# Two semaphores in turn for the second layer's gathers, each gather begun after the last but one has landed

## The reference, cut to what matters

```python
h = silu(edge_scalars @ Wfc1);  w = h @ Wfc2            # 192 weights of every edge
f0 = x0 @ Wl1_0;  f1 = einsum('num,uv->nvm', x1, Wl1_1) # 160 features of every node
e0 = f0[edge_src];  e1 = f1[edge_src]                   # the gather: a row of f for each edge
mid0 = w0 * e0 * sh0;   mid1 = w3 * (e1 . sh1);  mid2, mid3 = ...   # products
n0, n1, n2, n3 = segment_mean(mid, edge_dst)            # sums over the edges of a node
...                                                     # small products by node, layer norm
```

## Time and profile before

| | us |
|---|---|
| median of 3 runs | 6791.19 |
| lowest and highest of them | 6786.99, 6808.58 |
| span of the profiled execution | 6574.9 |
| PE busy (matmuls) | 4404.1 |
| DVE busy | 4082.6 |
| POOL busy | 3046.1 |
| ACT busy | 1176.2 |

### The profile page before, as it was taken

How to read it: one execution, slowest core, us unless ns; L and a number is a source line. 1 busy time by engine, 2 the same in 40 slices (tenths; PEclk the granted TensorE clock), 3 DMA queues, 4 the chain that set the end, 5 groups by cost and what they waited for, 6 DMA issues and landing times. The chain is left out here.

```text
span 6574.9 us, 113593 instructions
## 1 busy us (share of the span) xinstructions
PE 4404.1 (67%) x32521; PEld 3293.8 (50%) x32521; DVE 4082.6 (62%) x7506; ACT 1176.2 (18%) x3413; POOL 3046.1 (46%) x3249
## 2 busy tenths in 40 slices
PE   3767777777776777799776655655655665565555
PEld 2545555555555555689564434444444444444444
DVE  7877778778787766577455445444544544544544
ACT  0322222222222222000120111111111111111111
POOL 0556666566665666100035444444444444444442
PEclk7877778888788777899886666676666667666666
DMA  3333333333333333688332222222222222222221
GB/s 133 94 94 100 94 101 97 98 95 99 94 101 93 101 94 103 216 271 274 119 97 54 48 49 49 48 49 49 49 50 49 48 47 51 48 49 48 50 47 32
DMA packets 602395, 572.30 MB, mean 87 GB/s; under 512 B 183060, under 2 KB 491412, under 8 KB 602308
## 3 DMA queue, kind: packets, MB, share of 16 engines
q0 software_dynamic: 150528, 258.71, 14.5%
q1 hardware_dynamic: 414772, 227.28, 13.7%
q10 hardware_dynamic: 37008, 85.28, 4.2%
HBM read 412.44 MB, written 158.52 MB: 87 GB/s over the span
## 5 line engine op out<-in xcount | busy, mean ns | idle before, releaser
L2299 POOL DMA_INDIRECT q_fg<-f,q_index x1568 | 1484.1, 946 | 1608.8 <-DVE q_prod L2353 1138.1
L1026 POOL DMA_INDIRECT messages<-stage,place x1568 | 1506.8, 961 | 993.3 <-ACT stage L1237 506.4
L2546 PE MATMUL q_ps_m<-q_prod,q_onehot_sh 128*32 128x160 f32 x12544 | 914.4, 426 | 1015.6 <-DVE q_sums L2367 850.2
L1328 PEld LDWEIGHTS ps_m<-by_attr,turned 128*128 128x128 f32 x6272 | 1096.5, 226 | 281.3 <-issue 246.8
L2367 DVE SCALAR_TENSOR_TENSOR q_sums<-q_ps_m,split_q,q_sums 128x161 f32 x784 | 301.2, 384 | 1485.4 <-remote 1294.9
L1328 PE MATMUL ps_m<-by_attr,turned 128*128 128x160 f32 x6272 | 1204.7, 353 | 17.6 <-issue 13.0
L2546 PEld LDWEIGHTS q_ps_m<-q_prod,q_onehot_sh 128*32 128x32 f32 x12544 | 541.7, 150 | 1330.3 <-DVE q_sums L2367 908.4
L1298 PE MATMUL ps_y<-w_xy,xt 32*128 32x256 f32 (+3 forms) x1176 | 476.9, 705 | 488.0 <-ACT xz L1209 250.8
L2533 PE MATMUL q_ps_w<-q_wfc,q_hidden 64*128 64x192 f32 x3136 | 514.6, 425 | 206.6 <-DVE q_prod L2353 145.3
L1237 ACT COPY stage<-ps_m 128x320 f32<-128x320 f32 x784 | 337.2, 435 | 1737.9 <-PE ps_m L1328 848.1
L1118 DVE STREAM_TRANSPOSE by_attr<-by_node 128x2048 f32<-128x2048 f32 (+1 forms) x294 | 548.0, 1915 | 2.7 <-ACT by_node L1212 2.7
(11 more groups left out here) (247 smaller groups left out, 4487.3 us busy)
## 6 DMA issues: line engine op xcount, KB each, us to landing
nat<-in_edge_attr SPq DMA_DIRECT2D x392, 256.0 KB
rows_in<-messages ACTq DMA_DIRECT2D x208, 324.0 KB, 3.4
rows_in<-messages SPq DMA_DIRECT2D x208, 324.0 KB, 3.4
messages<-stage,place POOLq DMA_INDIRECT x1568
q_fg<-f,q_index POOLq DMA_INDIRECT x1568
messages<-zeros ACTq DMA_DIRECT2D x49, 324.0 KB, 2.2
q_a<-in_edge_attr SPq DMA_DIRECT2D x196, 64.0 KB
xw<-in_x SPq DMA_DIRECT2D x98, 80.0 KB
```

Source lines behind the costliest of these rows:

```text
L1026: nc.gpsimd.indirect_dma_start(out=msgs, out_offset=bass.IndirectOffsetOnAxis(ap=place[:, r, k:k + 1], axis=0), in_=stage[:, r, k, :], in_ ...
L1328: last = nc.tensor.matmul(ps_m[g % BANKS][:, k % 2 * D0:k % 2 * D0 + D0], turned[:, r, half, k * P:(k + 1) * P], by_attr[:, r, k, :, half] ...
L2299: nc.gpsimd.indirect_dma_start(out=fg[:, i, place_of(v), :], out_offset=None, in_=f_tab, in_offset=bass.IndirectOffsetOnAxis(ap=index[:, i ...
L2546: nc.tensor.matmul(ps_m[strip, 0:D0], oh_sh[:, strip], prod[:, h % 2, g * QUAD + place_of(v), 1 if c < 3 else 0, :], start=(v == 0), stop= ...
```

## The change

Two semaphores in place of eight, used in turn by the DMAs of a quad; each DMA waits until the one two before it has landed; the marker increment stands before each DMA; DVE and ACT wait for both semaphores, with counts that run through.

```diff
-            s_fg = [sem(f"fg{i}") for i in range(RING)]
+            INFLIGHT = 2
+            s_fg = [sem(f"fg{i}") for i in range(INFLIGHT)]
+            LANDS = 16 * (QUAD // INFLIGHT)
...
-                        pool.sem_inc(s_begun, 1)
                         for v in range(QUAD):
+                            reached(pool, s_fg[v % INFLIGHT], n * LANDS + v // INFLIGHT * 16)
+                            pool.sem_inc(s_begun, 1)
                             nc.gpsimd.indirect_dma_start(out=fg[:, i, place_of(v), :], out_offset=None, in_=f_tab,
-                                                         in_offset=bass.IndirectOffsetOnAxis(ap=index[:, i // 2, i % 2 * QUAD + v:i % 2 * QUAD + v + 1], axis=0)).then_inc(s_fg[i], 16)
+                                                         in_offset=bass.IndirectOffsetOnAxis(ap=index[:, i // 2, i % 2 * QUAD + v:i % 2 * QUAD + v + 1], axis=0)).then_inc(s_fg[v % INFLIGHT], 16)
...
-                        dve.wait_ge(s_fg[i], (t + 1) * (16 * QUAD))
+                        for landed in s_fg:
+                            dve.wait_ge(landed, (k * 2 + g + 1) * LANDS)
...
-                        for i in (2 * h, 2 * h + 1):
-                            reached(act, s_fg[i], t * (16 * QUAD))
+                        for landed in s_fg:
+                            reached(act, landed, (k - AHEAD + 1) * (2 * LANDS))
```

## The result

The changed kernel takes 6211.9 us (median of 4 runs, 6200.9 to 6217.9), the kernel before in the same comparison 6789.1 (6786.4 to 6808.6). The ratio is 0.9148, with a 95% interval of 0.9126 to 0.917: 8.5% faster, where slower was forecast. The profiled execution went from a span of 6574.9 to 6211.1 us, 363.8 us less.

What follows compares the result with a forecast made beforehand. Bound: the second layer's gather burst plus the chain behind it, PE's results coming at the latest with the last landing. Mean growth 1.69 us times 196 batches, 331 us, added to the median 6791.2 gave 7120; range 6420 to 7370.

Steps and rivals of the forecast that it cites:

- (1): Eight semaphores become two, with two waits each on DVE and ACT; taken as 0, 118 us at the most.
- (2): Marker increment on POOL moves from each quad to each gather, 1176 more sequencer instructions; taken as 0.
- (3): POOL's gather waits for landing of the one two before: 2.6 + 0.87 us, a pair 3.47 instead of 2.50.
- the 0.89 of the row: POOL's wake-up from a standing wait, read from message L2353's end to the gather's start; 0.87 us was used.
- Rival 2: POOL's wake-up is hidden, a pair takes 2.64 us; slower by 82 us at most, 6873; chance 0.09.
- rival 3: No change: no more than two or three gathers are under way, so the limit hardly binds; 6790; chance 0.06.
- (4): Second layer: PE stays late until the longer burst's last landing, 1.69 us per batch, 331 us; 7120, chance 0.48.
- rival 1: Second layer: pauses of 2.22 us free PE, batch falls to POOL's floor 13.88, 357 us less, 6434; chance 0.37.
- long batches: Second-layer batches of 18.79 us, whose add came with the last landing; claimed to grow by 2.91 us.
- short ones: Second-layer batches of 13.41 us, whose add came in mid-burst; claimed to grow only to POOL's floor, 0.47 us.
- 6950: Low end of the likeliest case: wake-up half hidden, pair of 3.0 us, long batches +1.5, short +0, 147 us.

Runs made afterwards that it cites:

- Four under way: The changed kernel with INFLIGHT 4 instead of 2, so each gather waits for the one four before; 5071.7 us, ratio 1.0025 to the kernel before.
- the bookkeeping stretch: Kernel before, second-layer rounds 8 to 14 of one execution, with an already-met wait and an extra increment ahead of each gather; 16.2 us a batch.

## Why the prediction was wrong

What bounds the kernel: right for the record, and only for sessions of its kind. "While gathers stream, PE's results are seen late" is what the runs confirmed; where it is not so, the same program takes 5059 us and POOL's 10.0 us a batch is the bound. That the trace of one execution can't tell this from a property of the program was not in the prediction at all.

(1) and (2), semaphores and increments at 0: right within what the runs can tell. Four under way costs 0.25% (13 us) where POOL is the bound; where PE is late the bookkeeping stretch is no faster than streaming.

(3), the price of the wait: right in size. A landing and a wake-up take 3.41 us (3.47), a pair 3.45 on the mean with 3.39 at the median (3.47), POOL's floor in the changed kernel is 13.79 (13.88). The wake-up is visible where it was disputed: with 2.6 us to the landing, 3.41 leaves 0.8 us, near the 0.89 of the row. The 50 ns that the Trainium skill gives ("DMA: Bandwidth & Descriptors", section "Anatomy of one DMA — SWDGE (gpsimd) path") are those of the sequencer's dispatch alone. They were no price for the whole way from a landing to the next gather's start, which is what the prediction used them for. Rival 2 is out by the same number, rival 3 by the pairs in the timeline.

(4), "held until the last landing", is the step that failed, and with it the choice between it and rival 1. Its arithmetic for a held batch is sound (570 us, the upper end of the forecast, when DVE was held in every batch), its premise is not: with the pairs, PE's results were not held, and DVE's waits for "remote" fell from 1295 us to 2.8. The split into long batches (+2.91) and short ones (+0.47), from which the 331 us came, was not tested. I decided between the two by one pause of 2.17 us in which PE crept on, and one of 2.68 in which it moved, as if the length of a single gap mattered. The gaps of the changed kernel are 2.1 us, the very length that I took for too short. But those of the earlier trace rows are single gaps in a stream of 1.25 us, the others come in each pair. In one execution a gap of 2.03 after each fourth gather fails and after each second succeeds, and by the table the mean spacing sorts the batches; the pairs' mean of 1.72 us lies over the boundary. The clue was in the prediction, as the last sentence of rival 1 (one gather under way where there had been two nearly all the time), and I gave it less weight than the two pauses. Two small slips changed nothing: the add of 5045.00 came just behind the start of the seventh gather (5044.98), so only the last had still to start, and 6791 + 147 is 6938, not 6950.

The size of rival 1 was right where its premises held: on the profiled span -357 us was computed and -364 came, in part by luck: the second layer gave -373, and +40 and -31 us came elsewhere. The predicted 6434 missed the measured 6211.9 for another reason: I added the difference to the median of 6791, which is 216 us above the time of the profiled execution. The changed kernel's median is within 1 us of its profiled run (6212.7). So the 216 us are not a constant around the span. The sessions with PE late gave the kernel before 6564.5, 6567.1 and 6762.6: it has two levels some 200 us apart, its profiled execution was at the lower and the timed runs of the record at the upper, and of the changed kernel only one level where PE is late is seen (6200.9 to 6217.9). Beside a kernel before of 6567 the same 6212 would be 5.4% faster instead of 8.5%, an estimate from two sessions. What makes the upper level is open.

The sign depends on what the prediction could not see: where PE is not late the same change costs 14.5%, by step (3) alone: (13.77 - 10.02) x 196 = 735 us, and 736 were measured (5795.9 - 5060.0).

No variant beats both kernels everywhere. Where PE is late, a write of 400 after each gather gave the shortest batch (12.65 us against 13.79 of the change), but as a whole kernel it ran only where PE is not late: 5562.0 us, better than the change's 5795.9 and 10% behind the kernel before.

## What to carry to other kernels

When results of one engine come late while another issues transfers, ask for the mean rate of the transfers as well as for the length of one gap, and read the answer where the rate itself differs. A limit on transfers under way sets a floor that can be computed before (landing plus wake-up for each group) and costs just that where nothing else was wrong; the waits for "remote" can be absent in another execution of the same kernel, so look at one before spending on them. That a stage stands at its floor does not say that the waits are gone: they may be covered. Add a difference to the time of the execution from which it was read, and treat a median that lies apart from it as a sign of a second regime.

## What was not expected of the hardware

One program, the kernel before, has three levels: about 5059, 6565 and 6763 to 6789 us. At the lowest, DVE and ACT see PE's results within some tenths of a microsecond and wait for nothing "remote"; at the others some come 7 us late and more while gathers stream (PE's sums are through at 5055.90, the add starts at 5062.70). The granted clock goes along (0.84 in the second layer against 0.67 in the earlier trace rows), but PE was idle more there, so this shows no direction. With gathers 1.58 us or more apart on the mean POOL runs at its floor; the lateness itself is nearly gone (0.4 us at the median) with evenly spaced gathers and with pairs, and is 1.8 to 2.1 us with four in a row. In the kernel before it is PE's updates of its semaphores that are recorded late, and not those of DVE and ACT. What links POOL's gathers to them, and what puts an execution on one level or another, no run here shows.
